# Graph layer on one core: early gathers from the raw node features, and a re-cut edge loop

## The reference, cut to what matters

```python
h   = maximum(layernorm(x), 0)                      # 12500 x 128
xp  = h @ lin1_w
C   = 0.5 * (cos(edge_weight * pi / 10) + 1)
W   = (ssp(edge_attr @ mlp_w1 + mlp_b1) @ mlp_w2 + mlp_b2) * C[:, None]   # 212500 x 128
agg = segment_sum(xp[src] * W, dst, 12500)
out = x + ssp(agg @ lin2_w + lin2_b) @ lin_w + lin_b
# ssp(v) = softplus(v) - log(2)
```

## Time and profile before

| what | value |
|---|---|
| time, median of 3 runs | 2168.35 us (2167.29 to 2168.58) |
| span of the profiled execution, first to last instruction | 2162.6 us |
| the profiled execution's own time | not listed apart; the median lies 5.75 us over the span |
| PE, PEld, DVE, ACT, POOL busy | 1804.4, 1331.3, 1433.5, 636.2, 1626.7 us |
| TensorE clock granted, mean | 0.779 of full speed |
| DMA | 175.95 MB, mean 81 GB/s |

### The profile page before, as it was taken

How to read it: one execution, slowest core, us unless ns; L and a number is a source line. 1 busy time by engine, 2 the same in 40 slices (tenths; PEclk the granted TensorE clock), 3 DMA queues, 4 the chain that set the end, 5 groups by cost and what they waited for, 6 DMA issues and landing times.

```text
span 2162.6 us, 28443 instructions
## 1 busy us (share of the span) xinstructions
PE 1804.4 (83%) x8534; PEld 1331.3 (62%) x8535; DVE 1433.5 (66%) x3688; ACT 636.2 (29%) x976; POOL 1626.7 (75%) x1742
## 2 busy tenths in 40 slices
PE   6888888888877888878888888888878888878887
PEld 6556666666655656656665666666656666655665
DVE  7867666666665666666666666666667666666665
ACT  6323232222222222222232222222322223222221
POOL 7877777777777777777777777777777777777775
PEclk9678787687787787887687877777778678788776
DMA  9322222222232222223232222222222222232221
GB/s 286 90 73 69 81 76 75 79 76 81 68 82 81 71 79 81 75 74 82 68 82 79 77 79 70 81 81 68 81 81 75 74 81 76 74 81 76 73 72 47
DMA packets 100170, 175.95 MB, mean 81 GB/s; under 512 B 29163, under 2 KB 67748, under 8 KB 94870
## 3 DMA queue, kind: packets, MB, share of 16 engines
q0 software_dynamic: 53152, 108.91, 18.0%
q1 hardware_dynamic: 46868, 65.22, 11.4%
HBM read 161.21 MB, written 12.80 MB: 80 GB/s over the span
## 4 chain that ended last, share of the span: by engine, by line
POOL 60%; issue 20%; PE 14%; DMA 3%; DVE 2%; DVEq 0%; ACT 0%; POOLq 0%; SPq 0%
POOL XG L307 59%; PE PW L619 4%; PE PA L631 4%; PE PX L605 3%; DMA XG<-xp_scratch,IX 3%; PE PW L617 1%; DVE SCR L403 1%; POOL TB L207 1%; DVE XG L509 1%; PE PF L648 0%; DVE MV L409 0%; PE PF L656 0%; PE PW L586 0%; DMA X<-x 0%; PE PX L573 0%
## 5 line engine op out<-in xcount | busy, mean ns | idle before, releaser
L307 POOL DMA_INDIRECT XG<-xp_scratch,IX x1661 | 1574.8, 948 | 507.4 <-issue 498.3
L371 ACT ACTIVATE TB<-TB 128x512 f32<-128x512 f32 x416 | 261.7, 629 | 1407.0 <-DVE TB L491 1406.9
L619 PEld LDWEIGHTS PW<-W,TB 128*128 128x128 f32 x3322 | 592.2, 251 | 21.4
L619 PE MATMUL PW<-W,TB 128*128 128x128 f32 x3322 | 594.5, 338 | 0.0
L509 DVE TENSOR_TENSOR XG<-PW,XG 128x512 f32<-128x512 f32 x416 | 286.2, 688 | 451.1 <-DMA XG<-xp_scratch,IX 448.1
L605 PE MATMUL PX<-AT,W 50*128 50x512 f32 x832 | 554.8, 752 | 7.1 <-DMA AT<-attr_t 7.1
L631 PEld LDWEIGHTS PA<-OH,XG 128*128 128x128 f32 x3322 | 544.4, 248 | 1.0 <-DVE XG L509 0.5
L631 PE MATMUL PA<-OH,XG 128*128 128x64 f32 x3322 | 543.3, 322 | 0.2 <-DVE AG L517 0.2
L617 PEld LDWEIGHTS PW<-BPB,ones 128*128 128x128 bf16 x416 | 41.3, 99 | 704.4 <-issue 649.6
L617 PE MATMUL PW<-BPB,ones 128*128 128x512 bf16 x416 | 195.2, 469 | 315.4 <-DVE XG L509 314.4
L491 DVE TENSOR_SCALAR TB<-PX,B 128x512 f32<-128x512 f32 x416 | 309.8, 745 | 202.9 <-PE PX L605 200.5
(11 more groups left out here) (73 smaller groups left out, 329.2 us busy)
## 6 DMA issues: line engine op xcount, KB each, us to landing
AT<-attr_t SPq DMA_DIRECT2D x103, 400.0 KB
XG<-xp_scratch,IX POOLq DMA_INDIRECT x1661, 2.5
X<-x SPq DMA_DIRECT2D x12, 512.0 KB, 7.4
xp_scratch<-XG SPq DMA_DIRECT2D x24, 256.0 KB, 4.4
out<-X SPq DMA_DIRECT2D x24, 256.0 KB, 5.2
IX<-src_t SPq DMA_DIRECT2D x1, 830.5 KB, 6.5
CC<-ew_t SPq DMA_DIRECT2D x1, 830.5 KB, 8.4
DI<-dst_t SPq DMA_DIRECT2D x1, 830.5 KB
```

What stands on the lines that cost most here:

```text
L307: e.indirect_dma_start(XG[q % XG_N][0:p, k * D:(k + 1) * D], None, xp, bass.IndirectOffsetOnAxis(ap=IX[0:p, t0 + k:t0 + k + 1], axis=0)).t ...
L371: e.activation(T[:, 0:w], T[:, 0:w], ACT.Exp).then_inc(s_ex, 1)
L619: ins = e.matmul(P[0:p, k * D:(k + 1) * D], TB[q % TB_N][:, k * TILE:k * TILE + p], W2[:, :], start=False, stop=(k == n - 1))
```

## The change

1. **POOL only gathers.** Its clears of AG and its share of the normalisation are gone. As its first work it gathers quads 0 to 13 (56 tiles) from `x` itself, with a first slice of the index table that SP loads ahead of everything else. It waits for the finished table before quad 14.
2. **14 more chunks.** The rows gathered raw are normalised, turned and multiplied as chunks 25 to 38, in place in `XG[0..13]`. Normalising is split: DVE subtracts the mean (`center`, one 128x512 operation on two SBUF operands), ACT relu comes behind the turn, and ACT multiplies by RS in `carry`, four 128x128 operations for a chunk.
3. **x is loaded into AG**, in 2 KB pieces (four consecutive rows a partition); AG is then cleared by a DMA of zeros, and the residual is loaded again for each closing chunk into a ring of four tiles `XR`.
4. **XG has 24 slots**; slots 14 to 19 serve as staging for the table. One semaphore for each slot in place of four.
5. **Edge loop.** b1 rides as a 51st row of w1 (a row of ones in `AT`). Even quads lie in partitions 0 to 50, odd ones in 64 to 114, and PE takes the pair in four alternating matmuls of 256 columns. Softplus is max(v,0) + ln(0.5 exp(-|v|) + 0.5): ACT takes |v| from PSUM, so DVE's clamp (L491) is gone. The one-hot matrices of a quad are one DVE operation (128x256, both operands in SBUF) without CC; CC goes into the message, now four DVE operations of 128x128. The scatter product is cut into two column halves of 64, and PA is one tile. DVE's order is: maximum, AG add, one-hot, message.

```diff
-    XG_N, TB_N, X1_N, OH_N = 6, 4, 3, 3
+    XG_N, TB_N, X1_N, OH_N = 24, 4, 4, 3
+    ST_N, XR_N = 6, 4
...
+        BATCHES = [0, 2, 6, 10, 14, 18, 22, NNC] + list(range(NNC + 4, NPC, 4)) + [NPC]
...
         @block.sync
+            e.dma_start(IX[:, 0:NR * QT], src_t[:, 0:NR * QT]).then_inc(s_i0, 16)
+            for j in range(len(XL) - 1):
...
             load(0)
-            e.wait_ge(s_x1, 1)
+            e.wait_ge(s_sub, NNC)
+            e.dma_start(AG[:, :], zero.partition_broadcast(128)).then_inc(s_az, 16)
             for k in range(1, AT_N):
                 load(k)
...
         @block.gpsimd
-            e.memset(AG[:, 0:AG0], 0.0).then_inc(s_ag, 1)
-            for c in range(NNC):
-                if c in BATCHES:
-                    e.wait_ge(s_nw, BATCHES.index(c) + 1)
-                norm(e, c, range(Y_POOL), s_yp)
-            e.memset(AG[:, AG0:], 0.0).then_inc(s_ag, 1)
+            e.wait_ge(s_i0, 16)
+            for q in range(NR):
+                t0, n, last = quad(q)
+                for k in range(n):
+                    e.indirect_dma_start(XG[q][:, k * D:(k + 1) * D], None, x,
+                                         bass.IndirectOffsetOnAxis(ap=IX[:, t0 + k:t0 + k + 1], axis=0)
+                                         ).then_inc(s_g[q], 16)
             e.wait_ge(s_ix, 16)
-            for i in range(XG_N):
+            for i in range(ST_N):
...
-            for q in range(NQ):
+            for q in range(NR, NQ):
...
         @block.scalar
+                for k, (o, m) in enumerate(parts(c)):
+                    ins = e.activation(to[0:m, o:o + D], PN[c % 4][0:m, o:o + D], ACT.Copy,
+                                       scale=RS[0:m, QT * c + k:QT * c + k + 1])
...
-                if 0 <= c - 1 < NNC:
-                    carry(c - 1)
+                if 0 <= c - 3 < NPC:
+                    carry(c - 3)
...
-                    e.wait_ge(s_cl, q + 1)
-                    e.activation(T[:, 0:w], T[:, 0:w], ACT.Exp).then_inc(s_ex, 1)
+                    e.wait_ge(s_x1, q + 1)
...
+                    e.activation(T[:, 0:w], PX[q % X1_N][:, 0:w], ACT.Abs).then_inc(s_ab, 1)
+                    e.wait_ge(s_ab, q + 1)
+                    e.activation(T[:, 0:w], T[:, 0:w], ACT.Exp, scale=-1.0).then_inc(s_ex, 1)
...
         @block.vector
+            def center(c):
...
+                    ins = e.tensor_tensor(TB[c % 4][0:m, a * D:b * D].rearrange("p (t d) -> p t d", d=D),
+                                          source(c)[0:m, a * D:b * D].rearrange("p (t d) -> p t d", d=D),
+                                          MV[0:m, QT * c + a:QT * c + b, 0:1].to_broadcast([m, b - a, D]),
+                                          ALU.subtract)
...
+            norms(0, NNC)
             e.wait_ge(s_tb, 16)
...
+            norms(NNC, NPC)
             e.wait_ge(s_sin, 1)
...
-            e.wait_ge(s_ag, 2)
+            e.wait_ge(s_bq, 6)
+            e.wait_ge(s_az, 16)
...
-                    for k in range(n):
-                        p = last if k == n - 1 else TILE
-                        ins = e.tensor_scalar(OH[q % OH_N][0:p, k, :], WI[0:p, 0:WIN], REL[0:p, t0 + k:t0 + k + 1],
-                                              CC[0:p, t0 + k:t0 + k + 1], ALU.is_equal, ALU.mult)
-                    ins.then_inc(s_oh, 1)
+                    e.tensor_tensor(OH[q % OH_N][0:p, 0:n, :], WI[0:p, 0:WIN].unsqueeze(1).to_broadcast([p, n, WIN]),
+                                    REL[0:p, t0:t0 + n].unsqueeze(2).to_broadcast([p, n, WIN]),
+                                    ALU.is_equal).then_inc(s_oh, 1)
...
+                    for k in range(n):
+                        G = XG[q % XG_N][0:p, k * D:(k + 1) * D]
+                        ins = e.scalar_tensor_tensor(out=G, in0=PW[q % 2][0:p, k * D:(k + 1) * D],
+                                                     scalar=CC[0:p, t0 + k:t0 + k + 1], in1=G,
+                                                     op0=ALU.mult, op1=ALU.mult)
+                    ins.then_inc(s_m, 1)
...
         @block.tensor
+                    turns = [(0, 0), (0, 1), (1, 0), (1, 1)] if w[1] == QE else [(0, 0), (1, 0), (0, 1), (1, 1)]
+                    for half, r in turns:
...
+                            K = slice(ODD * r, ODD * r + NG + 1)
+                            ins = e.matmul(PX[(q + r) % X1_N][:, a:b], W1[K, :], AT[k % AT_N][K, o + a:o + b],
+                                           start=(a == 0), stop=(b == w[r]))
...
-                        ins = e.matmul(PA[q % 2][:, 0:WIN], XG[q % XG_N][0:p, k * D:(k + 1) * D],
-                                       OH[q % OH_N][0:p, k, :], start=(k == 0), stop=(k == n - 1))
+                        for f in (0, D // 2):
+                            ins = e.matmul(PA[f:f + D // 2, 0:WIN], XG[q % XG_N][0:p, k * D + f:k * D + f + D // 2],
+                                           OH[q % OH_N][0:p, k, :], start=(k == 0), stop=(k == n - 1))
```

More of the change, by code:

```diff
@@ L129, in gnn_kernel @@
         s_b3 = sem("s_b3")
+        s_i0 = sem("s_i0")
         s_ix = sem("s_ix")
         s_dx = sem("s_dx")
-        s_xn = [sem(f"s_xn{i}") for i in range(13)]
+        s_xn = [sem(f"s_xn{i}") for i in range(14)]
         s_v = sem("s_v")
@@ L158, in gnn_kernel @@
         s_oh = sem("s_oh")
-        s_g = [[sem(f"s_g{i}_{k}") for k in range(QT)] for i in range(XG_N)]
+        s_g = [sem(f"s_g{i}") for i in range(XG_N)]
         s_m = sem("s_m")
+        s_ab = sem("s_ab")
         s_sc = sem("s_sc")
@@ L175, in gnn_kernel @@
         s_zg = sem("s_zg")
-        s_out = [sem(f"s_out{i}") for i in range(4)]
+        s_out = [sem(f"s_out{i}") for i in range(XR_N)]
+        s_xr = [sem(f"s_xr{i}") for i in range(XR_N)]
+        s_az = sem("s_az")
+        s_bq = sem("s_bq")
         def nodes(c):
@@ L251, in _ @@
                 if c >= 3 and c % 2 and tables:
-                    for _ in range(2):
+                    for _ in range(3):
                         if tables:
@@ L357, in _ @@
                     e.activation(ZT[c % 3][:, 0:w], PX[c % 3][:, 0:w], ACT.Relu).then_inc(s_re, 1)
-                if 0 <= c - 1 < NNC:
-                    carry(c - 1)
+                if 0 <= c - 3 < NPC:
+                    carry(c - 3)
+            e.wait_ge(s_b3, 1)
+            for k in range(3):
+                row = slice(32 * k, 32 * k + 1)
+                e.activation(BP[0][row, :].rearrange("p (n d) -> p n d", d=D),
+                             B16[k][row, 0:1, :].to_broadcast([1, QT, D]), ACT.Copy).then_inc(s_bq, 1)
+                e.activation(BP[1][row, 0:D], B16[k][row, 1, :], ACT.Copy).then_inc(s_bq, 1)
             e.wait_ge(s_cst, 1)
@@ L421, in newton, with norms @@
                 link(e.tensor_scalar(RV[:, t0:t1], RV[:, t0:t1], -0.5, 1.5, ALU.mult, ALU.add))
-                link(e.tensor_tensor(RS[:, t0:t1], RS[:, t0:t1], RV[:, t0:t1], ALU.mult))
-                link(e.scalar_tensor_tensor(out=RV[:, t0:t1], in0=MV[:, t0:t1, 0], scalar=-1.0,
-                                            in1=RS[:, t0:t1], op0=ALU.mult, op1=ALU.mult))
-                e.sem_inc(s_nw)
-            for step in range(NNC + 2):
-                if step < NNC:
-                    moments(step)
-                for b in range(len(BATCHES) - 1):
-                    if step == batch(b)[1] + 1:
-                        newton(b)
-                if 0 <= step - 1 < NNC:
-                    means(step - 1)
+                e.tensor_tensor(RS[:, t0:t1], RS[:, t0:t1], RV[:, t0:t1], ALU.mult).then_inc(s_nw, 1)
+            def norms(a, b):
+                for c in range(a, b):
+                    if c == 0:
+                        moments(0)
+                    means(c)
+                    if c + 1 < NPC:
+                        moments(c + 1)
+                    center(c)
+                    if c + 1 in BATCHES:
+                        newton(BATCHES.index(c + 1) - 1)
+            norms(0, NNC)
             e.wait_ge(s_tb, 16)
@@ L681, in fix @@
                 nc.gpsimd.sem_clear(s_zg)
-                nc.tensor.matmul(PX[0][:, 0:p], W1[:, :], AT[0][:, 0:p], start=True, stop=True)
+                nc.tensor.matmul(PX[0][:, 0:p], W1[0:NG + 1, :], AT[0][0:NG + 1, 0:p], start=True, stop=True)
                 nc.all_engine_barrier()
                 T = TB[0][:, 0:p]
-                nc.vector.tensor_scalar(T, PX[0][:, 0:p], B1[:, 0:1], CLAMP, ALU.add, ALU.min)
+                nc.scalar.activation(T, PX[0][:, 0:p], ACT.Abs)
                 nc.all_engine_barrier()
-                nc.scalar.activation(T, T, ACT.Exp)
+                nc.scalar.activation(T, T, ACT.Exp, scale=-1.0)
                 nc.all_engine_barrier()
@@ L800 @@
         "due": _np.array([512 * sum(done_by(c) < q for c in range(NNC - 1)) for q in range(NQ)], _np.float32),
+        "zero": _np.zeros((NWIDE * WIDE,), _np.float32),
+        "one": _np.ones((1, CHQ // 2 * QE), _np.float32),
         "win": _np.tile(_np.arange(WIDE, dtype=_np.float32), (TILE, 1)),
```

367 lines of the change are left out of this document (187 added, 180 removed).

## The result

| | before | after |
|---|---|---|
| median (range), us | 2168.47 (2167.29 to 2170.08), 4 runs | 2119.63 (2117.27 to 2122.22), 4 runs |
| ratio of the times | 1 | 0.9775, 95% interval 0.9761 to 0.9789 |
| profiled execution: time, span | 2162.6 (span) | 2117.27, 2115.5 |
| mean granted TensorE clock | 0.779 | 0.808 |

The change makes the kernel 48.8 us faster. The forecast was 2124.6, 5.0 us above the median. Between the two profiled executions the gain in span is 47.1 us (2162.6 to 2115.5) against a forecast of 43.7. The 5.75 us that I had carried over are not time around the span: the four runs after lie only 1.8 to 2.4 us over their own spans (2115.5 to 2120.3). Most of the 5.75 was the difference between the profiled execution before and the timed ones.

The account below looks back on a forecast made before the run. POOL's gathers with their issue gaps were taken to bound the kernel. The terms -64.7 + 10 + 1 + 0 + 10 gave -43.7 us, from 2168.35 to 2124.6 us, with a range of 2103 to 2140 at 0.70.

Parts of the forecast that it names:

- What bounds it: Whole kernel: POOL's 1,661 gathers with issue gaps, 1.249 us each, 5.00 us a quad, set the time.
- First gather: Kernel start: gathers begin at 3.3 us instead of 68.0, needing only an index slice, -64.7 us (bounds -65.1 and -62.9).
- POOL during the preparation: Early raw gathers: held by DVE's `center` (7.6 us) and other preparation work (2.4 us), +10 us, bounds 0 and 27.
- Table: Before quad 14: table ready at 75 to 78 us, 3 to 6 us ahead of POOL, +1 us (0 to +12).
- Ring: At gather 96: first scatter at some 121 us, before POOL needs slot 0 again at 132; 0 us (to +10).
- One-hot: Edge loop: two-operand one-hots hold gathers during catching up and closings, some 100 quads, +10 us (0 to 43).
- Consumers: Edge loop: savings on PE and DVE worth 0, covered by POOL's 5.00 us a quad; PE at worst 4.2 us.
- Outside the span: Around the profiled span: the same 5.75 us carried over from span to median time.
- Rival (a): Edge loop: one-hot locks onto a gather in every quad, up to 0.51 us a quad, 2198 to 2327 us; chance 0.12.
- (b): Preparation slips: table or slot 0 late by 10 to 25 us, 2135 to 2150 us; chance 0.10.
- (d): First 25 us: loading x fills the DMA engines and holds early gathers, 2145 to 2165 us; chance 0.03.
- (c): Edge loop: scatter's column halves run in turn, adding 2.6 us; PE bounds at 6.1 us a quad, 2.62 ms; chance 0.05.

Follow-up runs that it names:

- the moved one-hot: Kernel after with DVE's one-hot operation placed right behind the four message operations (q = i - 2 for i - 3): 2147.85 us, ratio 0.9927 to the kernel before.

## Why the prediction was right

- **What bounds it**: right for the condition under which the forecast was measured. The gathers with their issue gaps set the time before and after, and the consumers' savings were worth 0. Under the other condition the consumers set it.
- **First gather, -64.7**: measured -65.05. POOL waited 2.5 us for the index slice, as taken.
- **POOL during the preparation, +10**: measured +9.0. `center` came out as reckoned (6.96 for 7.6), by luck, since two errors cancel. Its phase was not random: a held gather takes 1.33 us, with its gap 1.63, and chunks came 1.63 us apart (14.64, 16.27), so gathers were held in series until a batch's small operations broke the rhythm. On the other hand the stretch that hits is shorter than the full length I used.
- **Table, +1**: +2.7, inside the bounds 0 to 12. The table was complete at 82.2, not at 75 to 78. ACT wrote the last rows, but it had idled 8.5 us before 75 us for `center`, which stood behind DVE's CK and bias work.
- **Ring, 0**: right. The first scatter was at about 125 us (forecast 121), and POOL was not held.
- **One-hot, +10**: the mechanism held and the size was off. Its length is 0.42, not 0.51, and only its first 0.29 us count. 30 gathers were held, 5.0 us. That it was so few is in part chance: in two versions with the same loop 64 were held, for 11.1 and 12.5 us. The old form was not quite free either (1.6 us).
- **Consumers, 0**: right in value, though the step put PE's need at 4.2 us a quad. It was 3.23 at a full clock.
- **Outside the span**: 1.8 to 2.4 us in every run after, in place of 5.75. The median of the four spans is 2117.5, 1.4 us under the forecast of 2118.9. So of the 5.0 us between forecast and median most is this term, and less is in the terms of the sum. The profiled execution alone lies 3.4 us under the forecast, above all by the loop term.
- **Rival (a)** did not occur, but the moved one-hot shows that it would have, at 0.10 us a quad and not 0.2 to 0.51. **(b)** and **(d)** did not occur in this condition: the gathers beside the load of x took 0.95 us where DVE did not hold them, and POOL had 13.57 us of work in the first 20. Under the other condition what (b) describes did happen, with a wait of 62.6 us for the table. **(c)** did not: PE's products ran side by side, the scatter's 6,640 took 357 us in all, the w1 products 294. Its price was read too high: 322 ns is the length of products that overlap. The 8 of a quad were busy for 1.3 us (542.7 for 415 quads), so 8 more one after another would add 1.3 and not 2.6, which makes 4.8 us a quad and does not decide.

The Trainium skill, SBUF — State Buffer, "Who interferes with whom", was borne out for the two-operand form. Beyond it the runs show when: only a gather that starts during the operation pays. That is why `center` and the one-hot cost 12 us together and not the 27 and 43 us of the upper bounds. The other rule weighed there, that `tensor_scalar` blocks GpSimd, was not borne out for forms this short: the four 128x64 forms held 18 of the gathers, 0.7 us in all, and the four 128x128 forms 11. They do hold a gather now and then. What keeps the price low is not their length alone, since most gathers that start during one of them are not held (13 of 87 were). A long one-operand form was not tried in the loop; L462 with its 1.03 us did hold a gather.

## What to carry to other kernels

When one engine's queue of equal steps sets the time, the gain is the idle time ahead of its first step; read there what it truly needs (here a 28 KB slice of indices and raw input), and count everything else at nothing. When an engine shares SBUF with it, ask for each operation not only how long it is but whether it is running when a step starts, and how many SBUF operands it has. Its place in the order, or a one-operand form in pieces, was worth more here than its total time; pieces of a two-operand form were not tried. And which engine sets the time can change with the condition of the machine: the same edit was 2.2% faster under one and 4.0% slower under the other. Time such a change under both.

## What the runs showed of the hardware that I had not expected

- A DVE operation that begins 0.06 us after a gather's start does it no harm; one that begins 0.16 us before (1013.76 for 1013.92) and runs 0.41 us holds it 0.14 us. A one-operand form of 128x64 that is running at the start mostly does no harm (13 of 87 gathers were held).
- PE's clock followed its waits: mean 0.78 of full speed with 1.8 us of slack a quad, 1.00 in 1,100 us in which it was busy for 1,099.4. A busy share read at a low mean clock says little about what room there is.
- The kernel before took 2165 us and 2523 us on one chip at different times. In the traces of the kernel after under the second condition, TensorE's semaphore updates came a median of 2.4 us behind the recorded end of their work while GpSimd gathered, and 0.02 us behind once it had stopped.

**Left open.** What the second condition is, and what makes the updates late in it. Whether NR = 16 or 17 with the one-operand forms beats 0.9745 under the first condition: it was measured only under the second, where it does not (1.0459 to 1.0468, behind the kernel after's 1.0400; why the one-operand forms cost 0.6% there was not found).
